# Rotary attention in a four-block transformer kernel: score and value products as three short-fp32 products, values for two tiles at a time

## The reference, cut to what matters

```
hd = 128
q, k, v = (einsum('bsd,hd->bsh', x, w) for w in (wq, wk, wv))
q, k = apply_rope(q), apply_rope(k)        # row 0 is left as it is
w = softmax(einsum('bqh,bkh->bqk', q, k) / sqrt(hd), axis=-1)   # no causal mask
out = einsum('bqk,bkh->bqh', w, v)
return einsum('bsh,dh->bsd', out, wo)
```

## Time and profile before

| | |
|---|---|
| median of 3 runs | 4145.25 us (4142.39 to 4164.42) |
| the profiled execution's own time | 4151.7 us |
| its span in the trace | 4150.0 us |
| mean granted TensorE clock | 0.978 of full speed |
| TensorE busy | 3930.1 us, 95% of the span |
| VectorE, ScalarE, GpSimd busy | 2798.7, 2639.6, 1556.3 us |
| rotary attention, first to last score product | 2416.4 to 2816.1 us |

### The profile page before, as it was taken

How to read it: one execution, slowest core, us unless ns; L and a number is a source line. 1 busy time by engine, 2 the same in 40 slices (tenths; PEclk the granted TensorE clock), 3 DMA queues, 4 the chain that set the end, 5 groups by cost and what they waited for, 6 DMA issues and landing times. The chain is left out here.

```text
span 4150.0 us, 65963 instructions
## 1 busy us (share of the span) xinstructions
PE 3930.1 (95%) x23476; PEld 2360.4 (57%) x23476; DVE 2798.7 (67%) x5635; ACT 2639.6 (64%) x3262; POOL 1556.3 (38%) x1303
## 2 busy tenths in 40 slices
PE   7999999999969999999999989997999999999999
PEld 4555545555457787887878855554444444444444
DVE  7978888888578878788787555444545555554553
ACT  2666666666765545455454334444888888888888
POOL 3222222222334445344353221111555455555545
PEclk8999999999979999999999999998999999999999
DMA  7543544444132232322323210005676766667674
GB/s 180 127 105 85 114 100 101 107 92 116 43 119 61 83 101 62 109 75 81 103 61 106 63 35 1 1 1 121 143 163 145 165 152 154 154 146 160 150 160 100
DMA packets 205762, 430.00 MB, mean 104 GB/s; under 512 B 47584, under 2 KB 72560, under 8 KB 189056
## 3 DMA queue, kind: packets, MB, share of 16 engines
q1 hardware_dynamic: 193360, 411.56, 41.0%
q0 software_dynamic: 4160, 6.35, 0.7%
q10 hardware_dynamic: 7920, 7.87, 0.6%
HBM read 338.59 MB, written 87.03 MB: 103 GB/s over the span
## 5 line engine op out<-in xcount | busy, mean ns | idle before, releaser
L2254 ACT ACTIVATE gelu_out<-hidden,b_col 128x1024 f32<-128x1024 f32 x1024 | 1054.5, 1117 | 182.9 <-PE hidden L2177 177.5
L2237 POOL TENSOR_TENSOR combined<-combined,gated 128x512 f32<-128x512 f32 x480 | 621.3, 1294 | 648.9 <-DVE gated L2354 473.2
L715 DVE TENSOR_REDUCE maxima<-front_and_scoresT 128x1 f32<-128x512 f32 (+3 forms) x1280 | 725.9, 630 | 79.5 <-PE front_and_scoresT L517 49.8
L615 ACT ACTIVATE probsT<-front_and_scoresT 128x1024 f32<-128x1024 f32 (+3 forms) x768 | 596.6, 811 | 263.7 <-PE front_and_scoresT L550 258.4
L1179 POOL TENSOR_TENSOR pair_sums<-sims 128x1024 f32<-128x1024 f32 x256 | 482.9, 1902 | 662.6 <-DVEq L1311 412.3
L2354 DVE SCALAR_TENSOR_TENSOR gated<-out_bank,b_col,gates_spread 128x512 f32<-128x512 f32 x480 | 360.3, 751 | 512.3 <-PE out_bank L2185 483.6
L2177 PE MATMUL hidden<-slice_stack,w_stack 128*128 128x512 f32 x2048 | 623.2, 428 | 37.9 <-ACT gelu_out L2254 37.8
L1107 PE MATMUL dense<-xnT,dense_weights 128*128 128x512 f32 x2304 | 537.3, 395 | 12.5 <-ACT silu_down L1213 8.6
L2177 PEld LDWEIGHTS hidden<-slice_stack,w_stack 128*128 128x128 f32 x2048 | 354.9, 190 | 327.0 <-ACT gelu_out L2254 249.6
L2185 PE MATMUL out_bank<-gelu_out,w_sb 128*32 128x512 f32 x4096 | 517.1, 607 | 3.2 <-DVE combined L2354 3.0
L1107 PEld LDWEIGHTS dense<-xnT,dense_weights 128*128 128x128 f32 x2304 | 434.9, 189 | 112.9 <-ACT silu_down L1213 9.2
(11 more groups left out here) (202 smaller groups left out, 5069.2 us busy)
## 6 DMA issues: line engine op xcount, KB each, us to landing
gates_spread<-gate_scratch SPq DMA_DIRECT2D x512, 256.0 KB, 5.4
dense_weights<-dense_scratch SPq DMA_DIRECT2D x384, 256.0 KB, 2.8
stack_scratch<-split_parts SPq DMA_DIRECT2D x192, 256.0 KB, 3.1
slice_stack<-slice_scratch SPq DMA_DIRECT2D x128, 256.0 KB, 8.1
q_stack<-stack_scratch SPq DMA_DIRECT2D x64, 384.0 KB, 6.2
k_stack<-stack_scratch SPq DMA_DIRECT2D x64, 384.0 KB, 9.2
slice_scratch<-slice_parts SPq DMA_DIRECT2D x32, 512.0 KB, 5.6
out_x<-x_tiles ACTq DMA_DIRECT2D x15, 512.0 KB, 2.9
```

The source lines that it names most:

```text
L615: nc.scalar.activation(PT[:, i % NPT, 2 * pr:2 * pr + 2, at:BANK], R[:, low:high + 1:high - low, at:BANK], ACT.Exp, scale=SCALE).then_inc( ...
L715: nc.vector.tensor_reduce(dst, bank(k)[:, 0:parts * w].rearrange("p (a k) -> p a k", a=parts), AX.X, ALU.max)\
L2237: nc.gpsimd.tensor_tensor(CM[:, par, hc, :], CM[:, par, hc, :], Y[:, u % 2, :], ALU.add)\
L2254: nc.scalar.activation(GH[:, k % GHB, :, :], HP[k % HPB][:, :, :], ACT.Gelu, bias=b1c[:, n % E:n % E + 1])\
```

## The change

Queries, keys, values and transposed probabilities are kept as a pair, a rounded high part and the remainder, both in the short type. Each fp32 product of the scores and of the value products becomes three short products that add up in PSUM. The high and low parts have to be made: for q and k ScalarE rounds the rotated sum (`high_part`) and GpSimd subtracts (a third operation in `rotate`); for the values VectorE copies and subtracts; for the probabilities ScalarE's copy now rounds, and VectorE reads the PSUM bank again and subtracts (`low_turned`). The groups of the value product become two tiles instead of four. `OT` has one buffer instead of two. The last part's weight is loaded in two halves through the buffer of this stage's raw weights and is split at steps 20 and 30.

```diff
-    GROUPS = [(4 * g, 4) for g in range(NT // 4 - 1)] + [(NT - 4, 2), (NT - 2, 1), (NT - 1, 1)]
+    GROUPS = [(2 * g, 2) for g in range(NT // 2 - 1)] + [(NT - 2, 1), (NT - 1, 1)]
-    SPLIT_AT = 20
+    SPLIT_AT = 20, 30
+    PARTS = ((0, 0), (0, 1), (1, 0))
...
-                    mm = nc.tensor.matmul(SC[n % 2][:, q * BANK:(q + 1) * BANK], QK[:, 0, b % 2, t * P:(t + 1) * P],
-                                          QK[:, 1, b % 2, q * BANK:(q + 1) * BANK], start=True, stop=True)
+                    for j, (of_q, of_k) in enumerate(PARTS):
+                        mm = nc.tensor.matmul(SC[n % 2][:, q * BANK:(q + 1) * BANK],
+                                              QK[:, of_q, 0, b % 2, t * P:(t + 1) * P],
+                                              QK[:, of_k, 1, b % 2, q * BANK:(q + 1) * BANK], start=(j == 0), stop=(j == 2))
...
                 for k in range(KT):
-                    mm = nc.tensor.matmul(OP[:, 0:size * P], V[:, b % 2, k, :], PT[:, g % 2, k, 0:size * P],
-                                          start=(k == 0), stop=(k == KT - 1))
+                    for j, (of_v, of_p) in enumerate(PARTS):
+                        mm = nc.tensor.matmul(OP[:, 0:size * P], V[:, b % 2, of_v, k, :], PT[:, g % 2, of_p, k, 0:size * P],
+                                              start=(k + j == 0), stop=(k == KT - 1 and j == 2))
...
                 pool.wait_ge(rc_ready, n)
-                nc.gpsimd.tensor_tensor(QK[:, SIDES.index(kind), b % 2, tok], RC[:, n % 2, :], SW[:, n % 2, :], ALU.add)\
+                nc.gpsimd.tensor_tensor(RC[:, n % 2, :], RC[:, n % 2, :], SW[:, n % 2, :], ALU.add).then_inc(rope_summed, 1)
+                pool.wait_ge(rope_high, n)
+                nc.gpsimd.tensor_tensor(QK[:, 1, SIDES.index(kind), b % 2, tok], RC[:, n % 2, :],
+                                        QK[:, 0, SIDES.index(kind), b % 2, tok].bitcast(F32), ALU.subtract)\
                   .then_inc(rope_ready, 1)
...
+            def high_part(kind, b, i):
+                n = r_count(kind, b, i)
+                act.wait_ge(rope_summed, n)
+                nc.scalar.activation(QK[:, 0, SIDES.index(kind), b % 2, i * BANK:(i + 1) * BANK], RC[:, n % 2, :], ACT.Copy)\
+                   .then_inc(rope_high, 1)
...
-                wait(act, y_done, y_count(GROUPS[g - 2][0] + GROUPS[g - 2][1] - 1) if g >= 2 else 0)
-                nc.scalar.activation(OT[:, g % 2, 0:size * P], OP[:, 0:size * P], ACT.Copy).then_inc(ot_ready, 1)
-
-            for kind, i in FRONT_FIRST:
-                if kind in SIDES:
-                    swap(kind, 0, i)
+                wait(act, y_done, y_count(GROUPS[g - 1][0]) if g else 0)
+                nc.scalar.activation(OT[:, 0:size * P], OP[:, 0:size * P], ACT.Copy).then_inc(ot_ready, 1)
+
+            for k, i in R_ORDER:
+                swap(k, 0, i)
+                high_part(k, 0, i)
             for n in range(STEPS):
                 for unit in front_units(n):
                     if unit[0] in SIDES:
                         swap(*unit)
                 if n < NT:
                     exps(n)
+                for unit in front_units(n):
+                    if unit[0] in SIDES:
+                        high_part(*unit)
                 if n in PV_AT:
                     keep_product(PV_AT[n])
                 for unit in turn_units(n):
...
-                nc.vector.tensor_copy(V[:, b % 2, 4 * i:4 * i + 4, :],
-                                      bank_of(("v", b, i))[:, :].rearrange("p (t h) -> p t h", t=4)).then_inc(v_ready, 1)
+                bank = bank_of(("v", b, i))[:, :].rearrange("p (t h) -> p t h", t=4)
+                high, low = (V[:, b % 2, part, 4 * i:4 * i + 4, :] for part in range(2))
+                nc.vector.tensor_copy(high, bank).then_inc(v_high, 1)
+                dve.wait_ge(v_high, v_count(b, i))
+                nc.vector.tensor_tensor(low, bank, high.bitcast(F32), ALU.subtract).then_inc(v_ready, 1)
+
+            def low_turned(unit):
+                _, n, i = unit
+                g = GROUP_OF[n]
+                at = n - GROUPS[g][0]
+                dve.wait_ge(pt_high, 2 * n + i + 1)
+                high, low = (PT[:, g % 2, part, 4 * i:4 * i + 4, at * P:(at + 1) * P] for part in range(2))
+                nc.vector.tensor_tensor(low, bank_of(unit)[:, :].rearrange("p (k q) -> p k q", k=4), high.bitcast(F32),
+                                        ALU.subtract).then_inc(pt_ready, 1)
...
                 for unit in front_units(n):
                     front(unit)
+                for unit in turn_units(n):
+                    low_turned(unit)
                 for unit in y_units(n):
                     stats(unit)
...
-    def split(self, dve, raw):
+    def split(self, dve, raw, k):
...
+        dve.wait_ge(self.half_in[k], 16 * self.G)
+        part = self.w1s[:, k * self.E // 2:(k + 1) * self.E // 2, :]
+        self.nc.vector.tensor_copy(part, raw[:, :, :]).then_inc(self.rounded, 1)
+        dve.wait_ge(self.rounded, k + 1)
+        self.nc.vector.tensor_tensor(part[low], raw[low, :, :], part[low].bitcast(F32), ALU.subtract)\
+            .then_inc(self.half_split, 1)
```

More of the change, by code:

```diff
@@ L1535, in rotary_attention @@
         XT = sb("xnT1", [P, DC, T])
-        QK = sb("turned_qk", [HD, 2, 2, T])
+        QK = sb("turned_qk", [HD, 2, 2, 2, T], F32R)
         RC = sb("rot_cos_part", [HD, 2, BANK])
         SW = sb("swapped_part", [HD, 2, BANK])
-        V = sb("values1", [P, 2, KT, HD])
+        V = sb("values1", [P, 2, 2, KT, HD], F32R)
         PQ = sb("probs", [P, 2, T])
-        PT = sb("probsT1", [P, 2, KT, 4 * P])
-        OT = sb("outT1", [HD, 2, 4 * P])
+        PT = sb("probsT1", [P, 2, 2, KT, 2 * P], F32R)
+        OT = sb("outT1", [HD, 2 * P])
         NMX = sb("neg_max1", [P, 2])
@@ L1545, in rotary_attention @@
         RZ = sb("recip_sum1", [P, KT])
-        W1R = sb("w1_raw", [P, later.E, later.I])
+        W1R = RAW[:, :, :].rearrange("p a d -> p (a d)").rearrange("p (e i) -> p e i", i=later.I)
         R = [ctx.enter_context(nc.psum_tensor(f"ring1_{i}", [P, BANK], F32)) for i in range(3)]
@@ L1561, in rotary_attention @@
         sin_ready = sem("sin1_ready")
+        rope_summed = sem("rope1_summed")
+        rope_high = sem("rope1_high")
         rope_ready = sem("rope1_ready")
@@ L1568, in rotary_attention @@
         t_done = sem("t1_done")
+        pt_high = sem("pt1_high")
         pt_ready = sem("pt1_ready")
+        v_high = sem("v1_high")
         pv_done = sem("pv1_done")
@@ L1605, in _ @@
         def _(sp):
+            sp.wait_ge(w_ready, 4)
             later.load(sp, W1R)
+            later.load_half(sp, W1R, 1)
         @block.tensor
@@ L1701, in out_projection @@
                     at = start + i - GROUPS[g][0]
-                    mm = nc.tensor.matmul(bank_of(unit)[:, i * D:(i + 1) * D], OT[:, g % 2, at * P:(at + 1) * P],
+                    mm = nc.tensor.matmul(bank_of(unit)[:, i * D:(i + 1) * D], OT[:, at * P:(at + 1) * P],
                                           WOT[:, :], start=True, stop=True)
@@ L1769, in keep_turned @@
                 wait(act, pv_done, g - 1)
-                nc.scalar.activation(PT[:, g % 2, 4 * i:4 * i + 4, at * P:(at + 1) * P],
+                nc.scalar.activation(PT[:, g % 2, 0, 4 * i:4 * i + 4, at * P:(at + 1) * P],
                                      bank_of(unit)[:, :].rearrange("p (k q) -> p k q", k=4), ACT.Copy)\
-                  .then_inc(pt_ready, 1)
+                  .then_inc(pt_high, 1)
             def keep_product(g):
@@ L1894, in _ @@
                     norms_ahead(n)
-                if n == SPLIT_AT:
-                    later.split(dve, W1R)
+                if n in SPLIT_AT:
+                    later.split(dve, W1R, SPLIT_AT.index(n))
 class MixtureWeights:
@@ L1921, in __init__ @@
         self.weights_in = ctx.enter_context(nc.semaphore("weights2_in"))
+        self.half_in = [ctx.enter_context(nc.semaphore(f"w1_half{k}_in")) for k in range(2)]
+        self.half_split = ctx.enter_context(nc.semaphore("w1_half_split"))
         self.rounded = ctx.enter_context(nc.semaphore("w1_rounded"))
@@ L1936, in load @@
             row = slice(self.HD * j, self.HD * (j + 1))
-            moves += [(raw[row, :, :], W1.rearrange("e d i -> d e i")), (self.b2c[row, :], b2.rearrange("e o -> o e")),
-                      (self.embd[row, j, :], emb)]
+            moves += [(self.b2c[row, :], b2.rearrange("e o -> o e")), (self.embd[row, j, :], emb)]
         self.all_in = 16 * len(moves)
@@ L1942, in load, with load_half @@
             sp.dma_start(dst, src, allow_slow_non_contiguous=True).then_inc(self.weights_in, 16)
-    def split(self, dve, raw):
-        low = slice(2 * self.HD, 4 * self.HD)
[L1947 to L1950, removed]
+        self.load_half(sp, raw, 0)
+    def load_half(self, sp, raw, k):
+        wait(sp, self.half_split, k)
+        experts = slice(k * self.E // 2, (k + 1) * self.E // 2)
+        for j in range(self.G):
```

(8 more changed lines are left out.)

## The result

The changed kernel takes 4263.77 us (median of 4 runs, 4257.64 to 4271.65), the kernel before 4143.86 us (4 runs). The ratio is 1.0286, with a 95% interval of 1.0264 to 1.0309: 120 us slower. The forecast was 4280, with 4200 to 4365 as the range. The profiled execution has a span of 4264.3 us and a mean granted clock of 0.965.

The account below looks back on a forecast made before the run. TensorE was taken to bound the stage before the change, with chained waits outweighing its lighter work after it. Terms 84 + 35 + 7 + 6 + 2 = 134 us on 4151.7 gave 4285.7, on the median's scale 4280; range 4200 to 4365.

Parts of the forecast that it names:

- The layout: Four-tile period written out per engine: TensorE idle 6.5 us before step 3's value product, period 31.95 us against 25.97.
- The term of 84 us: Waits in the stage: 6.0 us more per four-tile period, 14 times.
- the 2 for the split: Splitting the last part's weight in halves: 2 us, because VectorE has no slack at step 20.
- the x step's stop: In steps with x units TensorE stands 2.3 us, its transposes waiting for banks freed late.
- The clock: Half clock after stops: 2.5 us behind each of 14 long ones (35 us), 0.5 behind x-step stops (7 us).
- The opening: Start of the stage: chained swaps, rounding and GpSimd operations make the first exponential 6 us later.
- The last batch and its drain: Last batch, without fronts: 38.6 us for eight tiles, about the pace before, so no term.
- The rival of exposed loads: 256-wide short products pay their weight loads in full, 0.23 us each: 81 us more, 4360; chance 0.10.
- The rival in which the clock stays full: No slow clock behind the stage's stops: 4237 us; chance 0.15.
- the one with half the wait: The chain overlaps better and costs what the products give, or up to 60 us more; chance 0.10.
- The rival in which the gain arrives: ScalarE does not stand at q's high part, TensorE stays the late engine: faster, 4111 us; chance 0.09.

Follow-up runs that it names:

- The kernel with the filled stops: Changed kernel plus 24 extra 512-column short products, results thrown away, issued by TensorE in each of the 14 stops before a value product: 4248.32 us, ratio 1.0228.
- The best: Changed kernel with GpSimd, ScalarE and VectorE lists and the opening reordered, and in x steps the row maximum behind additions, x copies and low parts: 4127.75 us, ratio 0.9967.
- the opening in pairs: Opening with k and q swapped, then both rounded, one of four list moves made on the changed kernel: 4142.4 us, ratio 0.9998.

## Why the prediction was right

It held by its mechanism and, but for one term, by its sizes.

**Periods.** The layout gave the start of the value product 6.5 us of idle time, measured 6.0; ScalarE 4.1 us ahead of q's high part (9.7 to 13.8), measured 3.93; a period of 31.95 us at full clock. The kernel with the filled stops is the check of that: its usual period is 31.7, and its 14 periods (466.9 less the last, 19.6) average 31.95. The term of 84 us and the 2 for the split came out at 90.3 (447.3 less the 357.0 of the kernel before). About 4 of the 90.3 are still the clock, by the four stretches at 1.1 us each. That the remaining 86 are what was forecast is in part luck: the first period, which before holds no value product (19.4 us), had been counted like the others, 6.6 us too little loss, while the x step's stop was taken for 2.3 us and was 1.47, and the usual and the first period came out shorter than laid out.

**The clock.** 42 us were forecast and 26 measured. This is the term that was mis-sized. It has two parts. Behind the long stops, which I put at 2.5 us each, the value product lost 5.26 - 3.14 = 2.1 us where it is shown above, and 5.02 - 3.14 = 1.9 in the mean of all 14. This is the step that was off: I had counted the value product and the transposes behind it as slow, and the transposes at 2721.27 already ran at full clock (1.03 us for eight). The small stops in the x steps, which I took for 2.3 us with 0.5 for the clock, were 1.47 us. Behind six of the 14 the products were slow (the scores at 2728.72 took 2.79 us, those of the kernel with filled stops 1.64), and the usual periods vary between 33.6 and 34.6 us. With four such stretches left in the filled kernel, the whole clock term is nearer to 30 than to 26, as an estimate.

**The opening.** 6 us forecast, 5.2 measured (first maximum 24.3 and 29.5 us after the stage's first product).

**The last batch and its drain.** 0 forecast, 1.9 us gained (19.5 and 35.0 against 20.6 and 35.8).

**The sum.** With waits and clock parted as the filled kernel parts them, 90.3 + 26.1 + 5.2 - 1.9 = 119.7 against 134 forecast, and the stage measured by itself is 119.8 us longer. The median moved by 119.9. The spans of the two profiled executions differ by 114.3 only, because the one of the changed kernel entered the stage 5.4 us sooner, for reasons outside it.

**Short products.** 24 products of 256 columns took 3.03 us with the last one's tail, so 0.12 each as taken. The rival of exposed loads is gone. The Trainium skill, "TensorE: Matmul & The Clock Gate", Part 3, has it that a weight load overlaps running products only when it goes to another row group; the trace does not bear this out for this form, where full-array products with a load each are 0.12 us apart with 256 columns and 0.229 with 512. The rival in which the clock stays full is refuted by the windows above, and the one with half the wait by 14 stops of 6.0 us. The rival in which the gain arrives named the right switch: with ScalarE no longer held at q's high part, the stop was 0.9 us. But its 4111 was not reached by any order. The best gives 15 us of the 40: its usual period is 2.1 us shorter, not 2.5, there are 14 such periods and not 16, and the opening takes 11.7 us.

One reading of the prediction was too smooth: of the slices 23 to 27, which it has at nine tenths, the first and the last are at eight and seven. Nothing hangs on it.

Two of my expectations on the way were too low, 4129 for 4142 and 4111 for 4128, both for the same reason: they multiplied the usual period and left the first one and the periods with a split as they were. Why the opening in pairs did not shorten the opening (29.9 against 29.5) was not followed up.

## What to carry to other kernels

Cheaper products help only as long as the engine that makes them is the late one; before counting the gain, lay out one period with every engine's list in order, with the new conversions in it, and look for an engine that waits in the middle of its list with others' work behind it. A round trip between two engines (sum here, rounding there, subtraction here) costs its length twice when two units go through it one by one: put the first halves of both ahead of the second halves, and the round trip last in its step. Shorter groups may add to such a loss, but longer ones do not cover it: with groups of four and the score part alone, TensorE stopped for 4.7 us at its transposes in place of the value product.

## What the runs showed of the hardware that was not expected

Giving TensorE more to do made the kernel faster: 336 extra short products, 5.72 us of them in each stop, took 26 us out of the 14 periods, because the granted clock stayed at 1.00 (2.4 GHz) through the value products where an idle stop of 6.0 us had brought it to 0.50 (1.2 GHz). Shorter stops were followed by a slow value product, too: 4.40 us in place of 3.14 behind one of 3.94 us, and 5.49 us behind one of 3.21.
